# The small weights' loads on the other DMA queue, and a token mix whose first four groups do without the scale

## The chip, the cores and the metric

The kernel runs on one core of a Trainium2 chip. The core has five engines that run side by side and wait for each other by semaphores: TensorE (matmuls, into PSUM), VectorE, ScalarE, GpSimd and SyncE. SyncE (SP) computes nothing here and issues DMAs; ScalarE and GpSimd can issue DMAs too. The metric is the device time of one execution in microseconds. The kernel before takes 497.24 us, the median of 3 runs (497.1 to 499.32).

## The reference

The input x has 4 batches of 32 tokens, each an image of 128x128, float32. The layer is computed in two halves.

```
x1 = x + codano(ln_c(x), ...)           # ln_c: normalised along the last axis, eps 1e-6
out = x1 + ffn(ln_t(x1), W, V, ...)     # ln_t: the same with eps 1e-5

codano(x):  tokens = x as 128 images of one channel
  t = instance_norm(tokens)
  k, q, v = fno(t) with 16 heads        # 1x1 skip + spectral conv on the low modes
  p = softmax(q k^T / scale)            # 32x32 per batch and head
  a = fno(p v)                          # 16 heads -> 1 channel
  a = instance_norm(a + tokens)
  m = instance_norm(a)
  m = gelu(fno(m, norm)); m = fno(m, norm)
  return instance_norm(m) + a

ffn(x):  Wx = batch_norm(x W^T, gamma, beta)   # x as 4 x 16384 x 128
  y_t = sigmoid(Wx_t + V y_(t-1)), y_(-1) = 0   # a scan over 16384 steps
```

A Fourier transform along an axis is a matmul with cosines and sines. The whole of the path through attention and its skip is linear in the tokens once the softmax is known, so that for the pixels it is one 128x128 matrix over tokens, C (`cft` is its transpose), and instance norm multiplies each token's row of C by a scale alpha. The kernel calls the product of every pixel with alpha*C the token mix.

## The kernel before

The program is written out by hand as one block per engine, and what stands in a block is done in that order. Nothing is scheduled by a planner. The stages that matter here are these.

**First stage (span 0 to 78).** x is loaded in 8 chunks of 16 token rows (1 MB) on SP's queue (L472). VectorE takes each row's mean and variance (`ln_moments`, L1162), ScalarE the root (`root`, L947), VectorE the coefficients (`ln_coefs`, L1181, L1182, semaphore ln_coef). VectorE works on chunk c+1 before it gives the coefficients of chunk c. The rows are normalised in place, in each chunk some by ScalarE (L984: 12, 8 and then 4 rows) and the rest by GpSimd (L571: 4, 8 and then 12). TensorE multiplies the normalised rows with a Fourier basis (L625, semaphore rs_filled) and ScalarE copies the result to `rs` (`move_rs`, L388). SP writes the normalised rows to DRAM as xn_rows (L479), since later they are needed with tokens on the partitions; it waits there for both engines' normalised rows, and its queue is in order.

In the same time the weights are prepared. ScalarE issues 27 small DMAs first (L963 to L970); waits for six of them (w_in); scales the projection weights (L973); waits for four transposes of key and query weights and the transposes of W and V that TensorE has made (L977 to L979); and only then takes the first root. GpSimd copies the key and query weights (L539), waits for L973 (wy_skip) and multiplies value and projection weights (L556 to L566), before its first normalised row. The product goes to DRAM, wy_rows (L482), and comes back 16 times, spread over partitions (L488).

After the last chunk TensorE makes `rx`, the row spectra (L625, 128x512), that ScalarE and VectorE copy out (L388) into the place of x's chunks 4 and 5; for this they wait for the DMA that wrote these out (xn_4_5).

**Middle (78 to 139).** Low modes of all tokens, scores, softmax and the products of attention. TensorE fills its gaps with Gram matrices of the spectra: `low_gram` over 32 products, `gram(b, q0, q1)` over 32 per batch b. `gram(b, ...)` reads `rs` of batch b, in whose place xn_rows is read back as x_t, tokens on partitions (L510): chunks 2b and 2b+1, for which SP waits until batch b's Gram is whole (semaphore gram).

**Token mix (139 to 183).** VectorE gets the variance and asks ScalarE for a root (L945), and has alpha; it spreads it over partitions with a diagonal matrix `dg` (L1309) that TensorE multiplies with ones (semaphore bc_filled); `acft` = cft times alpha (L1314). For each of 32 groups of 4 tokens' columns, GpSimd (L584) or, in each fourth group, ScalarE (L1039) gathers the columns into one of five buffers, TensorE multiplies them with `acft` into one of PSUM's banks 4 to 7 (mix_filled), and ScalarE copies the bank to `a0` (L1053). Two things stand inside these 32 groups: TensorE waits behind group 3 for the diagonal of kappa (kap_dg, L1317), and ScalarE ahead of its copy of group 6 waits for zw, the mixer's product (L1322 to L1327 on VectorE), to square and sum it (L1049). From group 24 on TensorE also transposes z3_1.

**Rest (183 to 500).** The two mixers, the second normalisation, W, batch norm, and the scan.

## Time and profile before

| | us |
|---|---|
| median of 3 runs | 497.24 |
| profiled execution | 501.7 |
| its span, first to last instruction | 499.9 |
| TensorE busy | 360.9 (72%) |
| VectorE busy | 364.0 (73%) |
| ScalarE busy | 263.2 (53%) |
| GpSimd busy | 258.3 (52%) |

The profile is one execution. PE is TensorE, PEld its weight loads, DVE VectorE, ACT ScalarE, POOL GpSimd, SP SyncE; ACTq and SPq are the queues on which they issue DMAs. A line such as L571 is a line of the kernel before; matmuls pass through the helpers L625 and L629, and so all carry these. A float32 matmul counts as two passes in the rows' "x". The mean busy shares do not say which engine sets the end, since each stage has its own; the chain of waits does: it goes back from the last instruction, at each step to what released it. "[idle <-X]" at a row's end is the time in which the engine stood still before it, and who ended that.

### The profile page before, as it was taken

How to read it: one execution, taken by the hardware profiler on the slowest of the kernel's cores; microseconds unless marked ns; L12 is line 12 of the kernel's file. 1: busy time of each engine (PE TensorE's matmuls, PEld its weight loads, DVE VectorE, ACT ScalarE, POOL GpSimd, SP SyncE). 2: the span in 40 equal slices, each digit the busy share in tenths (PEclk: the TensorE clock that was granted, in tenths of full speed). 3: DMA queues.
4: the chain of work that ended last, by engine and by line, in shares of the span. 5: the costliest groups of instructions: out<-in, count | busy, mean ns of one | idle time of the engine just before them, and what ended most of it. 6: DMA issues, size and time to landing. Idle time of an engine off the chain costs nothing.

```text
span 499.9 us, 7077 instructions
## 1 busy us (share of the span) xinstructions
PE 360.9 (72%) x2385; PEld 281.8 (56%) x2385; DVE 364.0 (73%) x954; ACT 263.2 (53%) x530; POOL 258.3 (52%) x292
## 2 busy tenths in 40 slices
PE   0169989998949999899701956667865539697790
PEld 0169958794529998789701834333432227465690
DVE  3589312798967847999799477777778368899790
ACT  0678742520227854555100216888889948598000
POOL 1399940000039949997892567666772299300000
PEclk9989997999968999999955886998799978899796
DMA  8999893987150000035550000000000000000499
GB/s 209 272 305 276 227 304 105 208 314 319 26 207 1 1 1 1 1 112 161 167 155 17 1 0 0 3 0 0 0 2 1 0 1 0 1 2 0 127 286 261
DMA packets 61077, 50.93 MB, mean 102 GB/s; under 512 B 4897, under 2 KB 54481, under 8 KB 60017
## 3 DMA queue, kind: packets, MB, share of 16 engines
q1 hardware_dynamic: 57824, 50.18, 34.5%
q10 hardware_dynamic: 3216, 0.30, 0.6%
q8 instruction: 19, 0.31, 0.2%
q14 instruction: 18, 0.14, 0.1%
HBM read 30.45 MB, written 16.88 MB: 95 GB/s over the span
## 4 chain that ended last, share of the span: by engine, by line
DVE 38%; PE 29%; POOL 14%; ACT 7%; issue 5%; ACTq 3%; DMA 1%; DVEq 0%; SPq 0%
PE PS L625 26%; POOL BIG L571 7%; DVE PS L1475 7%; DVE BIG L1268 4%; DVE SML L1162 4%; PE PS L629 3%; DVE BIG L1443 3%; POOL BIG L611 2%; ACT BIG L1089 2%; POOL BIG L606 2%; ACT SML L388 2%; ACTq L970 2%; DVE SML L1457 2%; DVE BIG L1526 2%; DMA BIG<-xn_rows 1%
## 5 line engine op out<-in xcount | busy, mean ns | idle before, releaser
L625 PE MATMUL PS<-CST,BIG 128*128 128x128 f32 (+6 forms) x994 | 128.9, 322 | 23.4 <-ACT BIG L984 10.3
L625 PEld LDWEIGHTS PS<-CST,BIG 128*128 128x128 f32 (+1 forms) x994 | 114.1, 201 | 42.1 <-issue 12.8
L629 PE MATMUL PS<-CST,BIG 128*128 128x128 f32 (+1 forms) x326 | 54.5, 315 | 62.9 <-DVE BIG L1415 25.4
L629 PEld LDWEIGHTS PS<-CST,BIG 128*128 128x128 f32 (+1 forms) x326 | 44.2, 190 | 85.3 <-issue 54.7
L584 POOL COPY BIG<-BIG 128x512 f32<-128x512 f32 x24 | 30.5, 1324 | 77.6 <-DMA BIG<-xn_rows 74.5
L625 PE MATMUL PS<-BIG 128*128 128x128 f32 (+2 forms) x450 | 55.8, 375 | 2.6 <-DVE BIG L1268 2.1
L1162 DVE BATCH_NORM_STATS2 SML<-BIG 128x6 f32<-128x128 f32 x256 | 53.4, 279 | 5.7 <-DMA BIG<-in_x 4.4
L606 POOL TENSOR_TENSOR BIG<-BIG,SML 128x512 f32<-128x512 f32 x32 | 33.3, 1040 | 42.9 <-DVE SML L1182 27.9
L625 PE MATMUL PS<-BIG,SML 128*128 128x256 f32 (+3 forms) x214 | 48.4, 436 | 5.8 <-ACT BIG L1110 5.8
L388 ACT ACTIVATE BIG<-PS 128x512 f32<-128x512 f32 (+3 forms) x59 | 33.1, 572 | 34.2 <-PE PS L625 26.7
L625 PEld LDWEIGHTS PS<-BIG 128*128 128x128 f32 (+2 forms) x450 | 42.8, 175 | 13.2 <-issue 8.4
L1089 ACT ACTIVATE BIG<-BIG,SML 128x128 f32<-128x128 f32 x112 | 46.0, 482 | 3.8 <-DVE SML L1182 3.8
L596 POOL TENSOR_TENSOR BIG<-BIG 128x512 f32<-128x512 f32 x32 | 43.2, 1369 | 6.8 <-DMA BIG<-in_x 6.2
L1475 DVE SCALAR_TENSOR_TENSOR PS<-BIG,SML,PS 128x256 f32<-128x256 f32 x92 | 41.5, 489 | 5.3 <-PE PS L625 5.2
L625 PE MATMUL PS<-SML 128*128 128x512 f32 (+2 forms) x74 | 40.6, 643 | 4.5 <-DVE SML L1500 3.9
L625 PEld LDWEIGHTS PS<-BIG,SML 128*128 128x128 f32 (+1 forms) x214 | 31.2, 186 | 21.0 <-ACT BIG L1110 5.9
L618 POOL TENSOR_TENSOR BIG<-BIG,SML 128x512 f32<-128x512 f32 x32 | 31.9, 1039 | 17.3 <-ACT BIG L1089 17.3
L611 POOL TENSOR_TENSOR BIG<-BIG 128x512 f32<-128x512 f32 x32 | 40.6, 1271 | 0.0
L571 POOL TENSOR_SCALAR BIG<-BIG,SML 128x128 f32<-128x128 f32 x84 | 36.8, 447 | 0.0
L1121 ACT ACTIVATE BIG<-PS,SML 128x256 f32<-128x256 f32 x80 | 35.6, 473 | 1.1 <-DVE PS L1475 0.8
L590 POOL TENSOR_TENSOR BIG<-BIG,SML 128x512 f32<-128x512 f32 x32 | 32.0, 1034 | 7.0 <-ACT BIG L1053 7.0
L1443 DVE TENSOR_TENSOR BIG<-BIG,PS 128x512 f32<-128x512 f32 x32 | 21.7, 678 | 18.5 <-POOL BIG L611 16.9
(210 smaller groups left out, 541.6 us busy)
## 6 DMA issues: line engine op xcount, KB each, us to landing
xn_rows<-BIG SPq DMA_DIRECT2D x8, 1024.0 KB, 7.4
BIG<-xn_rows SPq DMA_DIRECT2D x8, 1024.0 KB, 8.0
BIG<-in_x SPq DMA_DIRECT2D x32, 256.0 KB, 3.0
out_x<-BIG SPq DMA_DIRECT2D x32, 256.0 KB, 3.6
BIG<-wy_rows SPq DMA_DIRECT2D x16, 192.0 KB, 5.4
BIG<-BIG SPq DMA_DIRECT2D x16, 192.0 KB, 4.0
BIG<-in_L_conv_mixer_w SPq DMA_DIRECT2D x2, 544.0 KB, 6.4
CST<-in_const SPq DMA_DIRECT2D x1, 547.5 KB, 8.8
```

Source lines behind the costliest of these rows:

```text
L388: return e.activation(o, i, ACT.Copy) if e is scalar_engine else e.tensor_copy(o, i)
L571: last = pool.tensor_scalar(x_h[:, n, :], x_h[:, n, :], ln_r[:, n:n + 1], ln_b[:, n:n + 1], ALU.mult, ALU.add)
L596: pool.tensor_tensor(v, v, stage[:, g % 3, :, :], ALU.add).then_inc(S("xa"), 1)
L606: pool.tensor_tensor(m1[:, v, :], m1[:, v, :], bet[:, v].unsqueeze(2).to_broadcast([128, 4, W]), ALU.mult).then_inc(S("bm1"), 1)
L611: pool.tensor_tensor(a0[:, v, :], a0[:, v, :], m1[:, v, :], ALU.add).then_inc(S("xm"), 1)
L625: return pe.matmul(o, l, rhs, start=start, stop=stop, **k)
L629: return pe.matmul(o, i, ident[0:n, 0:n], is_transpose=True, start=True, stop=True)
L1089: last = act.activation(m1[:, n, :], a0[:, n, :], ACT.Identity, scale=ln_r[:, n:n + 1], bias=ln_b[:, n:n + 1])
L1121: act.activation(at(y_s, g, i * 2 + (j0 + dj)), sums(g, dj), ACT.Sigmoid, bias=s("bb")).then_inc(S("state"), 1)
L1162: last = dve.bn_stats(ln_st[:, c % 2, row, :], src[:, XR * c + row, :])
L1443: TT(v, v, halves(4 + g % 4), ALU.add).then_inc(S("x1"), 1)
L1475: STT(sums(b, dj), wx_step[:, b, :, bass.ds(j, 1), :], s("bs"), sums(b, dj), ALU.mult, ALU.add).then_inc(S("vy_wx"), 1)
```

## The change

1. Of ScalarE's 27 loads four are left, the two skip weights first, then projection and value weights. The other 23 go to SP's queue: key, query, W and V behind x's chunk 2 (semaphore ffn_in), the 17 rows of parameters four at a time behind chunks 3 to 7, gamma and beta behind them, ahead of the second part of the constants.
2. GpSimd's copies of key and query weights move from its beginning behind chunk 3's rows, TensorE's six transposes behind chunk 4's products, ScalarE's copies of them behind the spectra of chunk 4.
3. The Gram semaphore counts halves of a batch, and SP reads x_t back chunk by chunk.
4. xlow's transposes stand behind 8 products of `low_gram`, not 14.
5. The mix's groups 0 to 3 are multiplied with `cft`, into banks 4, 5, 0 and 1, groups 0 and 1 ahead of TensorE's wait for `dg`. VectorE copies alpha (`al_bc`) and multiplies the four banks by it on their way to `a0` (a0_dve). Groups 4 to 31 go on as before with `acft`. The wait for kap_dg now stands behind group 4, and ScalarE's root of alpha stands ahead of its wait for x_t.

ScalarE's start before, in its own order: all loads stand ahead of the table load and of L973, which scales the projection weights.

```order
L963 DMA BIG<-in_L_conv_proj_w 16x1088
L963 DMA BIG<-in_L_conv_value_w 16x288
L963 DMA BIG<-in_L_conv_key_w 16x288
L963 DMA BIG<-in_L_conv_query_w 16x288
L963 DMA BIG<-in_L_conv_value_skip_w 16x1
L963 DMA BIG<-in_L_conv_proj_skip_w 16x1
...
L970 DMA BIG<-in_L_conv_value_skip_w 128x16
L970 DMA BIG<-in_L_conv_proj_skip_w 128x16
L973 ACT_TABLE_LOAD
L973 ACTIVATE BIG<-BIG 16x16x32 [waits w_in]
L973 ACTIVATE BIG<-BIG 16x16x32
L977 ACTIVATE BIG<-PS 128x64 [waits wt_filled]
```

And after:

```order
L987 DMA BIG<-in_L_conv_value_skip_w 16x1
L988 DMA BIG<-in_L_conv_proj_skip_w 16x1
L989 DMA BIG<-in_L_conv_proj_w 16x1088
L990 DMA BIG<-in_L_conv_value_w 16x288
L993 ACT_TABLE_LOAD
L993 ACTIVATE BIG<-BIG 16x16x32 [waits w_in]
L993 ACTIVATE BIG<-BIG 16x16x32
L978 ACT_TABLE_LOAD
L978 ACTIVATE SML<-SML 128x16 [waits root_of]
L1000 ACTIVATE BIG<-BIG,SML 128x128 [waits ln_coef]
L1000 ACTIVATE BIG<-BIG,SML 128x128 x11
L978 ACTIVATE SML<-SML 128x16 [waits root_of]
```

Gone from between are 23 loads and the three copies that waited for wt_filled; the first root (L978) follows L993 at once.

On SP's queue, before, eight loads of x followed each other, then the constants and the first three writes of normalised rows; the diff shows what now stands between them.

TensorE at the start of the mix before (each group is a row that waits and a row of three more):

```order
L625 MATMUL PS<-SML,CST 128x128 [waits dg]
L625 MATMUL PS<-SML,BIG 128x128 [waits x_mix_pool,acft]
L625 MATMUL PS<-SML,BIG 128x128 x3
L625 MATMUL PS<-SML,BIG 128x128 [waits x_mix_pool]
L625 MATMUL PS<-SML,BIG 128x128 x3
L625 MATMUL PS<-SML,BIG 128x128 [waits x_mix_pool]
L625 MATMUL PS<-SML,BIG 128x128 x3
L625 MATMUL PS<-SML,BIG 128x128 [waits x_mix_act]
L625 MATMUL PS<-SML,BIG 128x128 x3
L625 MATMUL PS<-SML,CST 128x128 [waits kap_dg]
L625 MATMUL PS<-SML,BIG 128x128 [waits x_mix_pool,a0]
L625 MATMUL PS<-SML,BIG 128x128 x3
```

And after:

```order
L643 MATMUL PS<-SML,BIG 128x128 [waits x_mix_pool,cx]
L643 MATMUL PS<-SML,BIG 128x128 x3
L643 MATMUL PS<-SML,BIG 128x128 [waits x_mix_pool]
L643 MATMUL PS<-SML,BIG 128x128 x3
L643 MATMUL PS<-SML,CST 128x128 [waits dg]
L643 MATMUL PS<-SML,BIG 128x128 [waits x_mix_pool]
...
L643 MATMUL PS<-SML,BIG 128x128 [waits x_mix_act]
L643 MATMUL PS<-SML,BIG 128x128 x3
L643 MATMUL PS<-SML,BIG 128x128 [waits x_mix_pool,a0_dve,acft]
L643 MATMUL PS<-SML,BIG 128x128 x3
L643 MATMUL PS<-SML,CST 128x128 [waits kap_dg]
L643 MATMUL PS<-SML,BIG 128x128 [waits x_mix_pool,a0_dve]
```

Two groups stand ahead of the wait for dg and two behind it, and the wait for kap_dg moved from behind the fourth group to behind the fifth.

On VectorE, the copy of alpha and the four multiplications stand between `acft` and the chain to kappa's diagonal; behind that come the six products that make zw.

The diff, without the lines around each place:

```diff
@@ -52,6 +52,7 @@
+WT_AFTER = 4
@@ -62,6 +63,7 @@
+MIX_EARLY = 4
@@ -243,6 +245,7 @@
+        al_bc = BIG3[:, 1664:1792]
@@ -343,6 +346,9 @@
+        def mix_bank(g):
+            return (4, 5, 0, 1)[g] if g < MIX_EARLY else 4 + g % 4
@@ -470,6 +476,17 @@
+                if c == 2:
+                    sp.dma_start(wcp[:, 1376:1664], t["key_w"].rearrange("o n h w v -> n (o h w v)")).then_inc(S("ffn_in"), 16)
+                    sp.dma_start(wcp[:, 1664:1952], t["query_w"].rearrange("o n h w v -> n (o h w v)")).then_inc(S("ffn_in"), 16)
+                    sp.dma_start(w_t, t["W"]).then_inc(S("ffn_in"), 16)
+                    sp.dma_start(v_t, t["V"]).then_inc(S("ffn_in"), 16)
+                if c >= 3:
+                    rows = [(n, *at) for n, at in ROW_AT.items() if at[1] <= NH]
+                    for name, a, size in rows[4 * c - 12:4 * c - 8]:
+                        sp.dma_start(PRM[:, a:a + size], flat(t[name]).to_broadcast([128, size])).then_inc(S("prm"), 16)
+            sp.dma_start(s("gamma"), t["gamma"].unsqueeze(1)).then_inc(S("gamma_in"), 16)
+            sp.dma_start(s("beta"), t["beta"].unsqueeze(1)).then_inc(S("gamma_in"), 16)
@@ -504,8 +521,7 @@
-                if c % 2 == 0:
-                    sp.wait_ge(S("gram"), c // 2 + 1)
+                sp.wait_ge(S("gram"), c + 1)
@@ -533,12 +549,8 @@
-            pool.wait_ge(S("w_in"), 16 * 6)
+            pool.wait_ge(S("w_in"), 16 * 4)
-            for k, (wt, part) in enumerate(((w_qry, 0), (w_qry, 1), (w_key, 0), (w_key, 1))):
-                last = pool.tensor_copy(qk_c[:, k, :, :], wt[:, :, 1:9, part].rearrange("n h w -> n w h"))
-            last.then_inc(S("qk_c"), 1)
@@ -572,6 +584,11 @@
+                if c == WT_AFTER - 1:
+                    pool.wait_ge(S("ffn_in"), 16 * 4)
+                    for k, (wt, part) in enumerate(((w_qry, 0), (w_qry, 1), (w_key, 0), (w_key, 1))):
+                        end = pool.tensor_copy(qk_c[:, k, :, :], wt[:, :, 1:9, part].rearrange("n h w -> n w h"))
+                    end.then_inc(S("qk_c"), 1)
@@ -583,7 +600,8 @@
-            pool.wait_ge(S("a0"), 32)
+            pool.wait_ge(S("a0"), 32 - MIX_EARLY)
+            pool.wait_ge(S("a0_dve"), MIX_EARLY)
@@ -634,16 +652,10 @@
-                if q1 == 32:
-                    last.then_inc(S("gram"), 1)
+                    if q % 16 == 15:
+                        last.then_inc(S("gram"), 1)
-            pe.wait_ge(S("ffn_in"), 16 * 4)
-            pe.wait_ge(S("qk_c"), 1)
-            for k in range(4):
-                tr(PS[:, 4, 16 * k:16 * k + 16], qk_c[:, k, :, :])
-            tr(PS[:, 5, 0:128], w_t)
-            tr(PS[:, 5, 128:256], v_t).then_inc(S("wt_filled"), 1)
@@ -656,6 +668,13 @@
+                if c == WT_AFTER:
+                    pe.wait_ge(S("ffn_in"), 16 * 4)
+                    pe.wait_ge(S("qk_c"), 1)
+                    for k in range(4):
+                        tr(PS[:, 4, 16 * k:16 * k + 16], qk_c[:, k, :, :])
+                    tr(PS[:, 5, 0:128], w_t)
+                    tr(PS[:, 5, 128:256], v_t).then_inc(S("wt_filled"), 1)
@@ -690,11 +709,11 @@
-            low_gram(0, 14)
+            low_gram(0, 8)
-            low_gram(14, 32)
+            low_gram(8, 32)
@@ -759,8 +778,24 @@
+            def mix(g, c):
+                if g % MIX_ACT == MIX_ACT - 1:
+                    pe.wait_ge(S("x_mix_act"), (g + 1) // MIX_ACT)
+                else:
+                    pe.wait_ge(S("x_mix_pool"), g + 1 - (g + 1) // MIX_ACT)
+                for w in range(4):
+                    last = mm(PS[:, mix_bank(g), 128 * w:128 * w + 128], x_mix[:, g % MIX_RING, w, :], c)
+                last.then_inc(S("mix_filled"), 1)
+            pe.wait_ge(S("cx"), 1)
+            mix(0, cft)
+            mix(1, cft)
+            mix(2, cft)
+            mix(3, cft)
@@ -782,17 +817,13 @@
-            for g in range(32):
-                if g >= 4:
-                    pe.wait_ge(S("a0"), g - 3)
-                if g % MIX_ACT == MIX_ACT - 1:
-                    pe.wait_ge(S("x_mix_act"), (g + 1) // MIX_ACT)
-                else:
-                    pe.wait_ge(S("x_mix_pool"), g + 1 - (g + 1) // MIX_ACT)
-                for w in range(4):
-                    last = mm(PS[:, 4 + g % 4, 128 * w:128 * w + 128], x_mix[:, g % MIX_RING, w, :], acft)
-                last.then_inc(S("mix_filled"), 1)
-                if g == 3:
+            for g in range(MIX_EARLY, 32):
+                if g < MIX_EARLY + 2:
+                    pe.wait_ge(S("a0_dve"), g - MIX_EARLY + 1)
+                if g >= MIX_EARLY + 4:
+                    pe.wait_ge(S("a0"), g - MIX_EARLY - 3)
+                mix(g, acft)
+                if g == MIX_EARLY:
@@ -805,7 +836,7 @@
-            pe.wait_ge(S("a0"), 32)
+            pe.wait_ge(S("a0"), 32 - MIX_EARLY)
@@ -953,30 +984,15 @@
-            for name, a, n, src in (
-                    ("w_in", 0, 1088, t["proj_w"].rearrange("n o h w v -> n (o h w v)")),
-                    ("w_in", 1088, 288, t["value_w"].rearrange("o n h w v -> n (o h w v)")),
-                    ("w_in", 1376, 288, t["key_w"].rearrange("o n h w v -> n (o h w v)")),
-                    ("w_in", 1664, 288, t["query_w"].rearrange("o n h w v -> n (o h w v)")),
-                    ("w_in", 1952, 1, t["value_skip_w"].rearrange("o n -> n o")),
-                    ("w_in", 1953, 1, t["proj_skip_w"])):
-                act.dma_start(wcp[:, a:a + n], src).then_inc(S(name), 16)
-            act.dma_start(w_t, t["W"]).then_inc(S("ffn_in"), 16)
-            act.dma_start(v_t, t["V"]).then_inc(S("ffn_in"), 16)
-            act.dma_start(s("gamma"), t["gamma"].unsqueeze(1)).then_inc(S("ffn_in"), 16)
-            act.dma_start(s("beta"), t["beta"].unsqueeze(1)).then_inc(S("ffn_in"), 16)
-            for name, (a, n) in ROW_AT.items():
-                if n <= NH:
-                    act.dma_start(PRM[:, a:a + n], flat(t[name]).to_broadcast([128, n])).then_inc(S("prm"), 16)
-            act.wait_ge(S("w_in"), 16 * 6)
+            act.dma_start(wcp[:, 1952:1953], t["value_skip_w"].rearrange("o n -> n o")).then_inc(S("w_in"), 16)
+            act.dma_start(wcp[:, 1953:1954], t["proj_skip_w"]).then_inc(S("w_in"), 16)
+            act.dma_start(wcp[:, 0:1088], t["proj_w"].rearrange("n o h w v -> n (o h w v)")).then_inc(S("w_in"), 16)
+            act.dma_start(wcp[:, 1088:1376], t["value_w"].rearrange("o n h w v -> n (o h w v)")).then_inc(S("w_in"), 16)
+            act.wait_ge(S("w_in"), 16 * 4)
-            act.wait_ge(S("wt_filled"), 1)
-            act.activation(aqk.rearrange("m k n -> m (k n)"), PS[:, 4, 0:64], ACT.Copy)
-            act.activation(w_t, PS[:, 5, 0:128], ACT.Copy)
-            act.activation(v_t, PS[:, 5, 128:256], ACT.Copy).then_inc(S("wt"), 1)
@@ -989,6 +1005,11 @@
+                if c == WT_AFTER + 1:
+                    act.wait_ge(S("wt_filled"), 1)
+                    act.activation(aqk.rearrange("m k n -> m (k n)"), PS[:, 4, 0:64], ACT.Copy)
+                    act.activation(w_t, PS[:, 5, 0:128], ACT.Copy)
+                    act.activation(v_t, PS[:, 5, 128:256], ACT.Copy).then_inc(S("wt"), 1)
@@ -1019,7 +1040,7 @@
-            act.wait_ge(S("gram"), 4)
+            act.wait_ge(S("gram"), 2 * NB)
@@ -1038,9 +1059,9 @@
+            root(s("al"), s("rt"))
-            root(s("al"), s("rt"))
@@ -1049,10 +1070,13 @@
-                act.wait_ge(S("mix_filled"), g + 1)
-                act.activation(a0[:, :, 4 * g:4 * g + 4],
-                               PS[:, 4 + g % 4, :].rearrange("h (w t) -> h t w", w=4), ACT.Copy).then_inc(S("a0"), 1)
+                if g >= MIX_EARLY:
+                    act.wait_ge(S("mix_filled"), g + 1)
+                    act.activation(a0[:, :, 4 * g:4 * g + 4],
+                                   PS[:, mix_bank(g), :].rearrange("h (w t) -> h t w", w=4), ACT.Copy).then_inc(S("a0"), 1)
+                    if g + MIX_ACT >= MIX_RING:
+                        act.wait_ge(S("mix_filled"), g + MIX_ACT + 1 - MIX_RING)
@@ -1312,6 +1336,11 @@
+            link(dve.tensor_copy(al_bc, PS[:, 6, 384:512]))
+            for g in range(MIX_EARLY):
+                dve.wait_ge(S("mix_filled"), g + 1)
+                TT(a0[:, :, 4 * g:4 * g + 4], PS[:, mix_bank(g), :].rearrange("h (w t) -> h t w", w=4),
+                   al_bc.unsqueeze(2).to_broadcast([128, NT, 4]), ALU.mult).then_inc(S("a0_dve"), 1)
@@ -1463,6 +1492,7 @@
+            dve.wait_ge(S("gamma_in"), 32)

```

## Rows read from the trace of the kernel before

**Rows 1.** The page, chain that ended last, shares by line:
```profile
PE PS L625 26%; POOL BIG L571 7%; DVE PS L1475 7%; DVE BIG L1268 4%; DVE SML L1162 4%; PE PS L629 3%; DVE BIG L1443 3%; POOL BIG L611 2%; ACT BIG L1089 2%; POOL BIG L606 2%; ACT SML L388 2%; ACTq L970 2%; DVE SML L1457 2%; DVE BIG L1526 2%; DMA BIG<-xn_rows 1%
```

**Rows 2.** The chain in order of time (start us, us, what):
```profile
14.98 0.72 ACTq L970
...
17.02 2.37 ACT BIG L973 x2
...
31.19 36.81 POOL BIG L571 x84
```

**Rows 3.** Timeline 0 to 60 (start us, us, engine, line):
```profile
3.06 0.44 ACTq L963 DMA_DIRECT2D BIG<-in_L_conv_proj_skip_w  x1
...
8.68 1.40 POOL L539 COPY SML<-BIG 16x128 f32<-16x128 f32 x4 [8.24 <-DMA BIG<-in_L_conv_proj_skip_w]
...
12.12 1.20 PE L629 MATMUL PS<-CST,SML 16*128 16x16 f32 x6 [12.12 <-DMA SML<-in_L_ffn_beta]
...
12.58 3.19 DVE L1162 BATCH_NORM_STATS2 SML<-BIG 128x6 f32<-128x128 f32 x16 [0.22 <-DMA BIG<-in_x]
...
21.95 4.74 ACT L984 ACTIVATE BIG<-BIG,SML 128x128 f32<-128x128 f32 x12 [0.53 <-DVE SML L1182]
...
28.46 3.19 DVE L1162 BATCH_NORM_STATS2 SML<-BIG 128x6 f32<-128x128 f32 x16
```

**Rows 4.** DMA: queue, issues (last: us to landing), issue times in ns, one issue:
```profile
q10 hardware_dynamic: 3216, 0.30, 0.6%
...
BIG<-in_x SPq DMA_DIRECT2D x32, 256.0 KB, 3.0
...
CST<-in_const SPq DMA_DIRECT2D x1, 547.5 KB, 8.8
...
L472 SPq DMA_DIRECT2D BIG<-in_x x8: 864/3374/4438, 1.3 to 25.6; - x8
...
9.54 0.96 ACTq L970 DMA_DIRECT2D BIG<-in_L_conv_mixer_out_g  x1
```

**Rows 5.** Timeline: a row of SP's queue, and ScalarE's first rx copy:
```profile
47.04 5.58 SPq L479 DMA_DIRECT2D xn_rows<-BIG  x2
...
71.08 0.60 ACT L388 ACTIVATE BIG<-PS 128x512 f32<-128x512 f32 x1 [1.07 <-PE PS L625]
```

**Rows 6.** Stretches: PE, PEld, DVE, ACT, POOL busy, PEclk, DMA, GB/s:
```profile
68.00:77.80 9.80, 8.79 (x46) 3.90 (x46) 3.64 (x10) 3.28 (x7) 0.14 (x1) 1.00 1.11 320
...
147.60:153.50 5.90, 5.88 (x31) 5.88 (x32) 5.49 (x11) 1.95 (x4) 3.74 (x1) 0.58 0.00 0
...
159.80:172.90 13.10, 13.10 (x120) 13.10 (x119) 8.45 (x8) 11.41 (x21) 13.10 (x12) 1.00 0.01 1
```

**Rows 7.** Timeline: Low Gram, scores, and the chain's last x_t landing:
```profile
82.74 5.91 PE L625 MATMUL PS<-BIG 64*128 64x128 f32 x28
...
96.63 3.64 PE L625 MATMUL PS<-BIG,SML 128*32 128x512 f32 x32
...
135.51 7.01 DMA BIG<-xn_rows
```

**Rows 8.** Timeline of alpha and the mix, and L1443 from the page:
```profile
143.93 0.75 DVE L1157 TENSOR_TENSOR SML<-SML,BIG 128x1 f32<-128x1 f32 x1
144.72 1.01 DVE L1309 TENSOR_SCALAR SML<-CST,SML 128x128 f32<-128x128 f32 x1
...
148.48 0.29 DVE L1317 TENSOR_SCALAR SML<-CST,SML 128x128 f32<-128x128 f32 x1
...
154.35 1.57 DVE L1327 TENSOR_TENSOR BIG<-BIG 128x512 f32<-128x512 f32 x1
...
156.35 1.05 ACT L1049 ACTIVATE BIG<-BIG 128x1024 f32<-128x1024 f32 x1
...
153.87 4.41 PE L625 MATMUL PS<-SML,BIG 128*128 128x128 f32 x38
...
L1443 DVE TENSOR_TENSOR BIG<-BIG,PS 128x512 f32<-128x512 f32 x32 | 21.7, 678 | 18.5 <-POOL BIG L611 16.9
```

## Prediction

> **What bounds the kernel now.** I read first the by-line shares of the chain of waits [rows 1]. TensorE's matmuls hold a quarter, but next stands one line of GpSimd, L571. So I opened the chain in order of time [rows 2]: ScalarE's queue issues small loads until 15.7, loads a table, scales the weights (L973, to 19.4), and only then GpSimd starts the weight products that occupy it up to 31.19. From there L571 runs 36.8 us with no gap. The end of the first stage (68.0) is therefore set by how early ScalarE gets through its queue, not by x. The timeline [rows 3] shows the same from the other side: VectorE has finished the statistics of chunk 1 at about 16.5 and starts chunk 2 only at 21.95, since the first root comes late on ScalarE. The second place of the change is the token mix. There TensorE has a queue of 256 passes; from 159.8 it is full (13.10 of 13.10 us), and before that it waits for alpha and then runs its first 32 passes at a granted clock of 0.58, the lower of its levels for most of the time [rows 6, 8].
>
> **The sum is made on the profiled execution:** span 499.9 us, 501.7 us measured. The median of the runs shown is 497.24, 0.9% lower; I take the differences over unscaled. All times below are on the clock of the trace before.
>
> **A. ScalarE's queue is cut to four loads.** An issue costs 0.44 us with 0.03 between, and six ended at 3.50 [rows 3], so with four ScalarE is through at 2.6, and the table load (1.28) is done by 3.9. L973 then waits for w_in. The skip weight, the slowest, now is issued first; before, GpSimd's copies that wait for the same loads started at 8.68, 5.6 after the last of them was issued at 3.06 [rows 3]. So it lands between 4.6 and 6.8; I take 6.8. L973 takes 2.37 -> 9.2. GpSimd's products take 31.19-19.46 = 11.7 -> 20.9, which is 10.2 earlier.
> GpSimd then needs coefficients. Chunk 0's are ready after VectorE's second chunk of statistics (12.58+3.19 and 0.8 of small operations, plus 0.5: 17.1), because x_in1 arrives at 12.5 [rows 3]. ScalarE normalises its 12 rows in 4.74, to 21.8, and gives root 1 behind them; VectorE's coefficients 1 stand at 22.6, and coefficients 2 one chunk later. A chunk takes VectorE 28.46 to 32.9, 4.4 us: 27.1. GpSimd, which would be ready for chunk 2 at 20.9+12x0.438 = 26.2, waits 0.9 us. From chunk 2 on 72 instructions of 0.44 (36.81/84) make 31.6, and the four copies of key and query weights, moved here in front of chunk 4, add 1.4 [rows 3]. GpSimd ends at 27.1+31.6+1.4 = 60.1; half a microsecond for VectorE's small operations waiting behind GpSimd's makes it 60.6. **Term A: -7.4.** Bounds: -8.8 (nothing waits after 20.9: 20.9+36.8+1.4 = 59.1) and -4.6 (L973 a further 2.8 late). The six transposes of key, query, W and V (1.20 us, at 12.12 before [rows 3]) move into TensorE's chunk 4; TensorE has two light chunks (6 and 7) behind it to catch up in, so I take 0 to 0.7, and 0.
>
> **B. SP's queue takes 23 loads between x's chunks.** Behind each stand x's next chunk, the second part of the constants, and the writes of the normalised rows. An x chunk takes SP 3.37 us to issue in the median but 0.86 when the queue is empty [rows 4], so SP is waiting for transfers already, and 2 to 4 issues of 0.45 fit into that wait. What they move is small: the whole ScalarE queue, 3216 packets, took 0.6% of the span, 3.0 us. VectorE needs chunks 4 to 7 at 27, 32, 36 and 40, and the eighth issue ended at 29.0 before; so even 21x0.47 = 9.9 us of pure delay lets GpSimd's later chunks through. What could suffer is the write of chunks 4 and 5, which the rx copies wait for. They are issued as GpSimd gets done with a chunk, the fourth at 47.04 [rows 5]. Now all come 7 us earlier, but the transfers of x and constants end no earlier than before (the last x issue started at 25.6 and took about 3.4, the constants follow and land 8.8 later: 37.8 [rows 4]). At the 320 GB/s of the stretch with the fullest queues [rows 6] a 1 MB write takes 3.3 us. Four of them bring the landing that releases the five wy loads to 51; with chunk 4, those loads (1 MB in all) and itself, chunk 5 lands at about 62; the rx copies want it at 71.08-7.4 = 63.7. Before, those copies waited for TensorE and not for the transfer [rows 5]. **Term B: 0**, up to +3.8 if the 9.9 us are not hidden (SP free at 43.6, chunk 5 landed at 67.5).
> The Trainium skill (DMA: Bandwidth & Descriptors, Issuing engines are not separate DMA queues) says that SP's and ScalarE's DMAs run on the same 16 engines and that a second issuer only saves issue time. By that rule the move costs x at most issue time; the 3.0 us of small packets are there either way.
>
> **C. Low Gram 8 instead of 14 first.** Six Low Gram products, 12 of 28 passes in 5.91 us, so 2.5 us, no longer stand ahead of xlow's transposes [rows 7]. But the same passes stand ahead of the score matmuls (96.63) in either order, and TensorE has hardly a gap up to there. **-0.2**, at most -2.5.
>
> **D. x_t in single chunks and the early mix.** Before, the last two chunks were issued together and were 7.0 us on their way, to 142.5 [rows 7]. Now only one is left for then. A 256 KB load lands in 3.0 [rows 4]; the slope from there to 2 MB in 7.0 is 2.3 us per MB. So x_t is complete at 140.1, not 142.5. GpSimd begins copying at 140.1, and that is while VectorE works out alpha. In the trace its operations with two SBUF inputs end on GpSimd's boundaries when a copy runs: the multiplication by g took 0.75 instead of 0.16, L1309 1.01 where L1317 took 0.29 [rows 8]. Copies from 140.1 on have their boundaries near 141.1, 142.1, 143.15, 144.2 and 145.2. VectorE's two updates of q end behind 142.1 and 143.15; then 0.15, the root 0.2 (it no longer stands behind ScalarE's column copy of 1.1) and the reciprocal 0.16, the product with g behind 144.2, the diagonal behind 145.2. Before it ended at 145.73: alpha is 0.5 earlier, and so is alpha*C (147.1).
> Then VectorE gets five operations more ahead of the kappa chain: the copy of alpha, 0.3, and four multiplications from PSUM of 0.68 (the 128x512 row of L1443, [rows 8]), 3.1 us with the links. Kappa's diagonal, at 148.77 before, is at 151.5. TensorE has done groups 0 to 4 by 149.8 and waits for it at group 4 (before it stood behind group 3 and cost nothing). Group 5 starts at 151.9, 2.9 earlier than before.
> The products that end in zw take 7.15 us after the diagonal: 158.7, not 155.9. **ScalarE waits for zw at group 6**, in its queue ahead of all further copies. Before, it arrived at 156.35, just as zw was there [rows 8]. Now it arrives 3 to 4 us too early and stands still: square 1.24, copies 6 and 7 1.07, columns of group 11 1.09 -> 162.1. TensorE starved for group 11 starts it at 162.1, where before it started at 160.2 (153.87, where group 4 began, and seven groups of 0.9). From there it is full as before (a group is 8 passes, 0.87 to 0.9). **Term D: +2.0.** Bounds: -5.1 (group 5 at 149.7 instead of 154.8 and no hold) and +5 (three more of VectorE's chained operations wait a full copy of 1.03).
> The Trainium skill (SBUF — State Buffer, SBUF: two separate sides) states an exclusive lock on the shared port pair for a whole instruction, against VectorE operations with two SBUF inputs. The trace agrees (0.75 and 1.01, above). Without such a lock alpha would be another 0.7 to 1.2 earlier and D about +1.
>
> **Sum:** -7.4 + 0 - 0.2 + 2.0 = -5.6. 497.24 - 5.6 = **491.6 us**. The rest of the kernel shifts as a whole; gamma and beta land hundreds of microseconds before they are read.
>
> **Rivals.**
> *The mix pays in full (chance 0.12).* If zw and kappa come in time, D is -5.1: -7.4-0.2-5.1 = -12.7, 484.5 us. For it: TensorE's 32 slow passes really leave the path. Against: the order of VectorE's queue, in which 3 us are put in front of zw.
> *The small loads hold x's stream (0.07), slower.* If a small load blocks SP's queue for the 0.96 us that some issues took on ScalarE's [rows 4], 21 of them add up to 20 us: SP is free at 52, the writes queue behind it, chunk 5 lands near 77 and the rx copies, at 71.1 before, end 4.1 later. With D +2.0 and C: +5.9, 503 us. It decides from a landing of chunks 4 and 5 at about 71. Against: those 0.9 rows stand for four of 27 loads, and SP's short first issue.
> *Both stages disappoint (0.15):* A -5, D +5, 497 us, no change that can be told. For it: many short chained operations of VectorE beside GpSimd.
> *B half hidden (0.13):* -7.4+3-0.2+2, 494.6.
> The forecast itself has 0.53, with 489 to 494.5 as its own range.
>
> **How the numbers follow.** About 0.5% (2.5 us) is what a measurement can tell from no change: below 494.75, above 499.7. Faster: nearly all of the forecast (0.50), the full mix 0.12, half of "half hidden" 0.07, 0.02 of the disappointment: 0.71. Slower: 0.07 and a tail of the disappointment, 0.09. Same: 0.20. The range goes from near the full mix to past the no-change case: 485.5 to 498.
>
> **What would show it.** A: L973 starts near 7, the run of 84 begins at 21 and ends at 60 to 61, with short waits for coefficients; if it ends after 63, A failed. B: SP's const issue ends before 36 and the rx copies again wait for TensorE; if they wait for xn_rows, B failed. D: x_t complete 2.4 us earlier relative to L1297's end; TensorE waiting for kappa's diagonal behind group 4; ScalarE waiting about 3 to 4 us for VectorE's zw before its square. If ScalarE does not wait there, the full mix is right. The forecast is wrong if the end of the mix (182.9 before) does not come 5 to 6 us earlier, or if a later stage takes another length.

## The result and the profile after

| | kernel before | changed kernel |
|---|---|---|
| median, first comparison | 498.13 (11 runs) | 494.37 (11 runs) |
| median, second comparison | 498.49 (16 runs) | 495.77 (12 runs) |
| profiled execution | 501.7 | 493.59 |
| its span | 499.9 | 491.8 |

The ratio is 0.9905 (95%: 0.9876 to 0.9933), and 0.9932 (0.9891 to 0.9973) in the second comparison: some 3.4 to 4.7 us faster. The ratios leave out executions that lie more than 1.5% above the fastest of the same kernel, which are two of 11 and two of 12 of the changed kernel's and six of 12 in experiment 4. 491.6 was predicted, from 497.24 for the kernel before.

The two profiled executions differ by 8.1 us, twice as much. To see what of this belongs to the change, stage boundaries were read from each trace of this study. "Scaling" is the start of the first scaling behind the residual Gram (L1000 before, L1021 after), "mask" the end of L1297 and L1321, "mix" the start of GpSimd's kappa products (L608 of the changed kernel), "bet" the start of its products with `bet` (L624), all in us; in brackets the time since the boundary on the left. Each is rounded by itself, so a difference can be off by 0.1.

| trace | scaling | mask | mix | bet | span |
|---|---|---|---|---|---|
| before, first | 82.9 | 140.6 (57.6) | 183.2 (42.7) | 280.1 (96.9) | 499.9 (219.8) |
| before, second | 81.9 | 137.2 (55.3) | 180.4 (43.2) | 275.7 (95.3) | 495.3 (219.6) |
| changed, first | 75.0 | 130.5 (55.5) | 177.0 (46.5) | 271.0 (94.0) | 491.8 (220.8) |
| changed, second | 75.6 | 132.9 (57.3) | 180.5 (47.6) | 276.7 (96.2) | 496.2 (219.5) |
| Low Gram split at 14 | 74.9 | 130.2 (55.3) | 175.5 (45.3) | 273.1 (97.6) | 493.7 (220.6) |
| no early mix | 74.6 | 130.1 (55.5) | 172.1 (42.0) | 269.4 (97.3) | 490.0 (220.6) |
| old start | 82.3 | 137.8 (55.5) | 185.3 (47.5) | 281.5 (96.2) | 501.0 (219.5) |
| ScalarE's waits later | 74.8 | 130.2 (55.4) | 170.8 (40.6) | 266.3 (95.5) | 486.9 (220.6) |
| all three waits later | 75.1 | 130.6 (55.5) | 172.0 (41.4) | 267.4 (95.4) | 486.8 (219.4) |

Up to the scaling the change gains 6.3 to 7.9 us (7.0 and 7.1 up to stage 2's first product, 69.89 and 69.76 before, 62.81 and 62.72 after). In the mix it loses 3.3 to 4.9 in these two pairs; the two other kernels with the same mix, those with the Low Gram split at 14 and with the old start, have 45.3 and 47.5, so that the loss over all four is 2.1 to 4.9. Between scaling and mask nothing but scatter lies. The traces scatter by more than the gain: the changed kernel's second one (496.2) ends 0.9 us behind the second one of before (495.3).

The start, in the timeline of the changed kernel (start us, us, engine, line, operation; in brackets the idle time before and who ended it). These answer to [rows 2, 3, 5]:

```profile
9.14 0.62 POOL L568 TENSOR_TENSOR BIG<-BIG 16x128 f32<-16x128 f32 x1 [8.70 <-ACT BIG L993]
...
20.80 1.80 POOL L583 TENSOR_SCALAR BIG<-BIG,SML 128x128 f32<-128x128 f32 x4
23.58 3.51 POOL L583 TENSOR_SCALAR BIG<-BIG,SML 128x128 f32<-128x128 f32 x8 [0.98 <-DVE SML L1206]
28.01 10.47 POOL L583 TENSOR_SCALAR BIG<-BIG,SML 128x128 f32<-128x128 f32 x24 [0.92 <-DVE SML L1206]
38.43 1.42 POOL L590 COPY SML<-BIG 16x128 f32<-16x128 f32 x4
39.84 21.07 POOL L583 TENSOR_SCALAR BIG<-BIG,SML 128x128 f32<-128x128 f32 x48
60.87 0.19 POOL L592 MEMSET BIG<- 128x128 f32 x1
...
62.81 3.65 PE L643 MATMUL PS<-BIG,CST 128*64 128x512 f32 x16 [0.57 <-ACT BIG L394]
64.23 0.60 ACT L394 ACTIVATE BIG<-PS 128x512 f32<-128x512 f32 x1 [1.29 <-DMA xn_rows<-BIG]
64.87 0.69 DVE L394 COPY BIG<-PS 128x512 f32<-128x512 f32 x1 [1.35 <-PE PS L643]
```

GpSimd's run of rows begins at 20.80 where it began at 31.19, 10.4 earlier. It now stands still twice for VectorE's coefficients (the first of them waited in turn 1.01 us for ScalarE's root, which stands behind ScalarE's 12 rows) and has the copies of key and query weights in it, so it ends at 60.9 where it ended at 68.0: 7.1 of the 10.4 are left. ScalarE's first rx copy now waits for the written rows and not for TensorE, 1.42 us behind the first product where before it was 1.19 (71.08 against 69.89). VectorE's first, at 64.87, still waits for TensorE, so the 0.2 us go no further.

SP's queue of the changed kernel (the third column names the queue; what the row shows is the time until it had issued), which answers to [rows 4]:

```profile
8.07 3.51 SPq L480 DMA_DIRECT2D BIG<-in_L_conv_key_w  x1
...
13.20 0.71 SPq L478 DMA_DIRECT2D BIG<-in_x  x1
13.95 1.97 SPq L487 DMA_DIRECT2D BIG<-in_L_conv_norm_g  x1
15.96 0.43 SPq L487 DMA_DIRECT2D BIG<-in_L_conv_attn_norm_g  x1
...
30.84 0.71 SPq L478 DMA_DIRECT2D BIG<-in_x  x1
31.59 2.34 SPq L487 DMA_DIRECT2D BIG<-in_L_conv_proj_skip_w  x1
...
34.92 0.43 SPq L490 DMA_DIRECT2D CST<-in_const  x1
```

The time that x's chunks used to take to issue (3.37 in the median) has passed to the first small load behind each of them (1.6 to 3.5 us); the chunk itself takes 0.71, the other small loads 0.43. The constants start to be issued 5.9 us later than before, at 34.92, and their issue ends at 35.35 where it ended at 32.82. Nobody misses them, and from x's third chunk on VectorE waits for x in neither kernel.

The token mix of the changed kernel, its timeline from alpha on, for [rows 8]:

```profile
129.87 6.09 POOL L601 COPY BIG<-BIG 128x512 f32<-128x512 f32 x6 [68.81 <-DMA BIG<-xn_rows]
...
134.00 1.02 DVE L1333 TENSOR_SCALAR SML<-CST,SML 128x128 f32<-128x128 f32 x1
...
137.09 2.48 DVE L1342 TENSOR_TENSOR BIG<-PS,BIG 128x512 f32<-128x512 f32 x4
...
141.23 0.28 DVE L1346 TENSOR_SCALAR SML<-CST,SML 128x128 f32<-128x128 f32 x1
...
141.57 0.49 PE L643 MATMUL PS<-SML,CST 128*128 128x128 f32 x2 [1.70 <-DVE SML L1346]
141.89 4.63 PE L643 MATMUL PS<-SML,BIG 128*128 128x128 f32 x40
...
143.01 7.98 POOL L601 COPY BIG<-BIG 128x512 f32<-128x512 f32 x4 [2.03 <-PE PS L643]
...
147.09 1.53 DVE L1356 TENSOR_TENSOR BIG<-BIG 128x512 f32<-128x512 f32 x1
148.66 1.06 ACT L1070 ACTIVATE BIG<-BIG 128x1024 f32<-128x1024 f32 x1 [5.07 <-DVE BIG L1356]
...
150.34 7.85 PE L643 MATMUL PS<-SML,BIG 128*128 128x128 f32 x42 [3.82 <-ACT BIG L1075]
```

ScalarE stands 5.07 us at its square of zw, VectorE's last product before it being L1356. Its copies of groups 6 and 7 stand behind the square, and TensorE's group 10 needs the bank of group 6. TensorE has eaten what ScalarE had emptied for it, stands 3.82 us, and resumes at 150.34. What it resumes with is in the stretches (engines in the order of [rows 6], then the granted clock):

```profile
141.90:146.50 4.60, 4.60 (x42) 4.43 (x40) 4.57 (x5) 0.60 (x1) 3.49 (x1) 1.00 0.00 0
150.30:155.00 4.70, 4.66 (x22) 4.66 (x23) 1.03 (x4) 3.74 (x7) 1.51 (x2) 0.50 0.00 0
155.00:160.00 5.00, 5.00 (x40) 5.00 (x40) 2.02 (x5) 3.70 (x7) 3.49 (x4) 0.86 0.00 0
160.00:176.00 16.00, 16.00 (x146) 16.00 (x146) 10.07 (x12) 11.74 (x19) 9.48 (x9) 1.00 0.01 3
```

Behind the idle time TensorE runs at 0.50, the lower of its levels (1.2 GHz): 22 passes in 4.66 us, 0.21 each, where it needs 0.11 at full clock.

The length of this hold is not the same in each execution. In the second trace of the changed kernel two of VectorE's six products took 2.0 us instead of 1.1, beside GpSimd's copies, and ScalarE stood longer:

```profile
146.06 2.00 DVE L1353 TENSOR_TENSOR BIG<-BIG 128x512 f32<-128x512 f32 x1
...
152.89 1.06 ACT L1070 ACTIVATE BIG<-BIG 128x1024 f32<-128x1024 f32 x1 [6.79 <-DVE BIG L1356]
```

In the first trace L1353 was short:

```profile
143.56 1.10 DVE L1353 TENSOR_TENSOR BIG<-BIG 128x512 f32<-128x512 f32 x1
```

Over the four traces with this mix ScalarE stood 4.0, 5.1, 6.8 and 6.8 us, TensorE behind it 2.2, 3.8, 5.5 and 5.5, and the mix took 45.3, 46.5, 47.5 and 47.6: the longer the hold, the longer the mix.

### The profile page after: what moved, and what is told of

The parts are those of the page before. It is cut to its first block, busy times and chain, and to the rows that moved or that the text cites. A ratio compares the mean times of both kernels' runs of the same rounds, so it can differ in the third digit from the quotient of the medians.

```text
span 491.8 us, 7081 instructions
## 1 busy us (share of the span) xinstructions
PE 358.8 (73%) x2385; PEld 279.8 (57%) x2385; DVE 365.3 (74%) x959; ACT 260.8 (53%) x526; POOL 258.5 (53%) x292
## 4 chain that ended last, share of the span: by engine, by line
DVE 42%; PE 28%; POOL 13%; ACT 9%; issue 4%; DMA 1%; DVEq 0%; SPq 0%; ACTq 0%; POOLq 0%
PE PS L643 24%; DVE PS L1505 7%; POOL BIG L583 6%; DVE BIG L1292 6%; DVE SML L1186 5%; PE PS L647 4%; ACT BIG L1113 3%; DVE BIG L1472 2%; POOL BIG L608 2%; ACT SML L394 2%; POOL BIG L629 2%; DVE BIG L1556 2%; POOL BIG L624 2%; DVE SML L1486 2%; DMA BIG<-in_x 1%
## 5 line engine op out<-in xcount | busy, mean ns | idle before, releaser
L643 PE MATMUL PS<-CST,BIG 128*128 128x128 f32 (+6 forms) x994 | 126.5, 319 | 31.4 <-ACT BIG L1000 19.9
L643 PEld LDWEIGHTS PS<-CST,BIG 128*128 128x128 f32 (+1 forms) x994 | 111.5, 197 | 49.9 <-issue 32.7
L647 PEld LDWEIGHTS PS<-CST,BIG 128*128 128x128 f32 (+1 forms) x326 | 44.5, 189 | 81.4 <-issue 53.5
L643 PE MATMUL PS<-BIG 128*128 128x128 f32 (+2 forms) x450 | 53.5, 368 | 2.6 <-DVE BIG L1292 2.1
L624 POOL TENSOR_TENSOR BIG<-BIG,SML 128x512 f32<-128x512 f32 x32 | 33.3, 1042 | 40.0 <-DVE SML L1206 27.9
L394 ACT ACTIVATE BIG<-PS 128x512 f32<-128x512 f32 (+3 forms) x59 | 32.4, 571 | 29.8 <-PE PS L643 21.5
L643 PEld LDWEIGHTS PS<-BIG 128*128 128x128 f32 (+2 forms) x450 | 40.6, 168 | 13.0 <-issue 8.2
L636 POOL TENSOR_TENSOR BIG<-BIG,SML 128x512 f32<-128x512 f32 x32 | 32.0, 1041 | 17.3 <-ACT BIG L1113 17.3
L629 POOL TENSOR_TENSOR BIG<-BIG 128x512 f32<-128x512 f32 x32 | 40.6, 1271 | 0.0
L643 PE MATMUL PS<-SML,BIG 128*128 128x128 f32 (+1 forms) x264 | 35.4, 298 | 5.2 <-ACT BIG L1075 3.8
L643 PEld LDWEIGHTS PS<-SML,BIG 128*128 128x128 f32 (+1 forms) x264 | 34.3, 213 | 6.2 <-ACT BIG L1075 4.0
```

The costliest lines, as they stand in the source:

```text
L394: return e.activation(o, i, ACT.Copy) if e is scalar_engine else e.tensor_copy(o, i)
L624: pool.tensor_tensor(m1[:, v, :], m1[:, v, :], bet[:, v].unsqueeze(2).to_broadcast([128, 4, W]), ALU.mult).then_inc(S("bm1"), 1)
L629: pool.tensor_tensor(a0[:, v, :], a0[:, v, :], m1[:, v, :], ALU.add).then_inc(S("xm"), 1)
L636: pool.tensor_tensor(a0[:, v, :], a0[:, v, :], g0[:, v].unsqueeze(2).to_broadcast([128, 4, W]), ALU.add).then_inc(S("x1_g0"), 1)
L643: return pe.matmul(o, l, rhs, start=start, stop=stop, **k)
L647: return pe.matmul(o, i, ident[0:n, 0:n], is_transpose=True, start=True, stop=True)
```

## Experiments

All ratios are against the kernel before, run beside them on the same chip. The first four share one set of its runs (median 498.01 of 29), the next four another (498.49 of 16), the last four a third (498.76 of 11).

**1. The Low Gram split undone.** `low_gram(0, 14)` and `low_gram(14, 32)` again.

> The changed kernel with one part undone: the Low Gram passes are again split at group 14, as in the kernel before; the new start and the early mix stay. The changed kernel was 4.7 us faster than the one before, and its trace gained 3.0 us between the first residual copy and the mask (10.08 us ahead there, 7.08 at stage 2's start), where the prediction had 0.2. Theory: the reorder made these 3 us, by keeping TensorE supplied while the clock of the kernel before fell to 0.56 at 77.8 to 88.4 us. Then this kernel loses 2.5 to 3 us against the changed one (ratio to before 0.995 to 0.997) and its trace shows a granted clock under 0.9 in the Low Gram. Rival: the dip belonged to that one execution or to other work (DMA), then this kernel stays within 0.5 us of the changed one (ratio 0.990) at a clock near 1.0 there.

Measured: 0.9941 (0.9918 to 0.9964), median 495.13. The two theories give 0.996 and 0.990, and the time lies between them; the traces decide. Scaling to mask takes 55.3 us with the split at 14 and 55.5 with 8. TensorE in that kernel:

```profile
74.77 3.58 PE L643 MATMUL PS<-BIG 64*128 64x128 f32 x28
```

The 28 passes take 3.58, where they took 5.91 in the first trace of before [rows 7]. The reorder is not what saved the time. What this kernel has over the changed one in its trace is a stretch at half clock elsewhere, after the mix (0.50 from 180 to 190, 97.6 us to `bet` against 94.0). Its median is 0.8 us over the changed kernel's in the first comparison and 0.6 under it in the second.

**2. The early mix undone.** Alpha's root stands behind ScalarE's first column copy, all 32 groups are multiplied with `acft`, VectorE's five operations are gone.

```diff
-            link(dve.tensor_copy(al_bc, PS[:, 6, 384:512]))
-            for g in range(MIX_EARLY):
...
-                if g == MIX_EARLY:
...
+                if g == 3:
                     pe.wait_ge(S("kap_dg"), 1)
```

> The changed kernel with the early mix undone: alpha's root stands behind the mix's columns again, the first four groups are multiplied with the diagonal that kappa is in, nothing is scaled at the copies; the new start, x transposed by chunk and the Low Gram split at 8 stay. Theory: the early mix costs 2 to 4 us (the trace of the changed kernel lost 3.8 us between the mask and the mix's end), so this kernel is 2 to 4 us faster than the changed one: 486 to 488 where before has 497, ratio 0.980 to 0.985. It keeps the earlier landing of x_t (2.7 us between mask and GpSimd's copies). Rival: the early groups are worth what they fill of TensorE's wait, then this kernel is slower than the changed one by 1 to 3 us, ratio 0.993 to 0.997.

Measured: 0.9866 (0.9814 to 0.9917), median 491.4. In the trace the mix takes 42.0 us instead of 46.5 and 47.6, so the early mix costs 4.5 to 5.6 (3.3 against the shortest of the four traces that have it). ScalarE's wait at the square is 1.3 us, not 5.07, though two of VectorE's products were long here too. By the ratios the time falls only by 2 to 3. This trace has a stretch at half clock behind the mix (0.50 from 175 to 185, 97.3 to `bet`); whether the other executions had one is not known. The ratio lies just above the 0.980 to 0.985 expected.

**3. The old start.** All loads on ScalarE, key and query weights first on GpSimd, the rest as in the changed kernel.

> The changed kernel with the start of the kernel before: all small loads on ScalarE's queue, q and k copied and transposed ahead of x's statistics; x transposed by chunk, the Low Gram split at 8 and the early mix stay. Theory: the start is worth 7.1 us, handed on undiminished, so this kernel is 7 us slower than the changed one: 1.5 to 3 us slower than before, ratio 1.003 to 1.006 (early mix +3.8 us and middle -3 us against before, if the middle's gain is the reorder's, so down to 1.000). Rival: part of the start's gain is given back later (x's last groups waited for), then this kernel is only 4 to 5 us slower than the changed one, ratio 0.998 to 1.001.

Measured: 1.005 (1.0012 to 1.0088), median 501.44: by the ratios 5.9 to 7.2 us over the changed kernel. GpSimd's run and all behind it are where they were:

```profile
31.50 36.77 POOL L576 TENSOR_SCALAR BIG<-BIG,SML 128x128 f32<-128x128 f32 x84
```

The scaling starts at 82.3 against 75.0. The start's 7.1 us are handed on whole. And what is left of the change without it is by the ratio 2.5 us slower than before (0.6 to 4.4): the price of the mix's term in the time itself.

**4. All three waits later.** ScalarE's and TensorE's.

```diff
-                if g == MIX_EARLY:
+                if g == MIX_EARLY + 4:
                     pe.wait_ge(S("kap_dg"), 1)
...
-                if g == 6:
+                if g == 11:
                     act.wait_ge(S("zw"), 1)
...
-                if g == 14:
+                if g == 17:
                     root(s("r1"), s("rt"))
```

> The changed kernel with its early mix kept and three waits put where what they wait for is ready: ScalarE's square of zw behind group 11 of the first product's copies (was 6), its root behind group 17 (was 14), and TensorE's wait for kappa's diagonal four groups later, so that eight groups are multiplied with C alone before the queue stands (was four). Theory: what the early mix costs is these holds (ScalarE stood 5.07 us at the square, TensorE 3.82 us, and ran at a granted clock of 0.50 for the 4.7 us behind it). Without them the mask-to-mix-end stretch is 4 to 6 us shorter than in the changed kernel: 487 to 489 where before has 497, ratio 0.979 to 0.984, and the clock behind the diagonal stays above 0.8. Rival: the mix is bound by VectorE's chain to kappa's and zw's ends, whatever stands in the queues, then this kernel is within 1 us of the changed one, ratio 0.989 to 0.992.

Measured: 0.987 (0.9822 to 0.9919), above the 0.979 to 0.984 expected. Its 12 times lie between 487.1 and 499.8 with a median of 493.99, so the time alone is unclear. The mix takes 41.4 us in the trace, 5 less than in the changed kernel, as expected. ScalarE still stands 3.44 us at its square, and the granted clock is 1.00 behind the diagonal but 0.77 from 147 to 152. Groups 4 to 8 are multiplied with `acft` here too; what moved is TensorE's wait alone.

**5. The kernel before, profiled again.**

> The kernel before, unchanged, profiled a second time. In its first profile 56.4 us passed from the first of the six scalings behind the residual Gram (82.9 us) to the mask's end; in the changed kernel, with the Low Gram split at 8 or at 14, and with the old start and the split at 8, it was 53.9 to 54.3 us, and none of these four shows the granted clock under 1.0 between 78 and 88 us (there 0.66). Theory: the fall of the clock there was an event of that one execution; then this profile has 54.1 us in that stretch, a clock of 1.0 at 78 to 88 us, and if it falls elsewhere the 3 us are lost there; time 496 to 499. Rival: the old start together with the split at 14 brings the fall each time; then it is here again, at 56.4 us.

Measured: 497.11 us, within the 496 to 499 expected. TensorE in the middle of this second trace, beside [rows 7]:

```profile
81.75 3.58 PE L625 MATMUL PS<-BIG 64*128 64x128 f32 x28
```

and its stretch there:

```profile
77.00:87.00 10.00, 9.54 (x82) 9.10 (x81) 3.25 (x9) 3.88 (x13) 0.00 (x0) 1.00 0.27 69
```

In the first trace of the same kernel that stretch was:

```profile
78.00:88.00 10.00, 10.00 (x58) 9.62 (x59) 1.10 (x5) 2.93 (x9) 0.00 (x0) 0.66 0.17 36
```

The clock is 1.00 instead of 0.66, and scaling to mask takes 55.3 instead of 57.6. From stage 2's first product (69.76) to the mask it is 67.5 us, in the first trace 70.6, in the changed kernel 67.7. So all of the 3.0 us that the first pair of traces seemed to gain there belongs to that one execution of the kernel before. Against this second trace the changed kernel's first is 3.5 us ahead at the end, near the 3.8 and 2.7 of the medians.

**6. The changed kernel again.**

> The changed kernel, unchanged, on this chip again, to set the others of this call against and for a second trace. Expected ratio 0.990 with an interval that overlaps the first one (0.988 to 0.993). If TensorE's half clock falls in at a place that differs from execution to execution, this trace's milestones agree with the first within 0.5 us up to the mask and differ by 2 to 4 us where a fall lies (175 to 190 us, as in two other kernels, or none); if the place belongs to the kernel, both traces agree throughout.

Measured: 0.9932 (0.9891 to 0.9973), median 495.77. Its trace shows the same event in the same place:

```profile
70.00:78.00 8.00, 7.55 (x47) 6.96 (x45) 1.20 (x7) 2.39 (x8) 0.00 (x0) 0.74 1.09 307
78.00:88.00 10.00, 10.00 (x77) 9.76 (x76) 8.01 (x7) 6.82 (x20) 0.00 (x0) 0.87 0.79 168
```

57.3 us from scaling to mask, 1.8 over the others, with the Low Gram split at 8. So the clock can fall in this stretch with either split, and mostly does not: in two of the nine traces of the table, and in none of the other five there. My expectation that the two traces would agree up to the mask was wrong. Counted from stage 2's first product to the mask, the two cost 3.2 us (70.7 against 67.5) and 2.6 (70.2 against 67.7). The stretches behind the mix in experiments 1 and 2 are such events in another place; what they cost can't be told as well, since from mix to `bet` the traces without them have anything from 94.0 to 96.9.

**7. ScalarE's two waits alone.** As 4, without the edit on TensorE.

> The changed kernel with ScalarE's two waits alone moved (square of zw behind group 11 of its copies, was 6; root behind 17, was 14); TensorE's wait for kappa's diagonal stays behind group 4. With all three moved the stretch from the mask to the mix's end took 41.4 us against 46.5 in the changed kernel. Theory: ScalarE's hold (5.07 us at the square, TensorE without work 3.82 us behind it and at half clock for 4.7 us) is most of it: 42 to 43 us here, and the time 2 to 4 us under the changed kernel's. Rival: TensorE's own hold of 1.7 us at the diagonal, with the late refill behind it, is what counts: then 45 us or more.

Measured: 0.9808 (0.9746 to 0.9869), median 488.55. The mix takes 40.6 us, less than the 42 to 43 expected, and the time is by the ratios 4.8 to 6.2 us under the changed kernel's, where 2 to 4 were expected. It is also less than the 41.4 with all three waits moved, but experiment 12 has 40.4 for that kernel, so moving TensorE's wait too shows neither gain nor loss. The timeline of this kernel:

```profile
140.71 0.49 PE L643 MATMUL PS<-SML,CST 128*128 128x128 f32 x2 [1.83 <-DVE SML L1346]
...
141.03 19.66 PE L643 MATMUL PS<-SML,BIG 128*128 128x128 f32 x160
...
148.71 1.05 ACT L1070 ACTIVATE BIG<-BIG 128x1024 f32<-128x1024 f32 x1
```

TensorE still waits 1.83 us for kappa's diagonal, but from 141.03 on runs 160 passes without a break, and ScalarE comes to its square without waiting. Its stretches:

```profile
141.00:145.00 4.00, 4.00 (x23) 4.00 (x23) 3.97 (x5) 1.45 (x3) 2.21 (x1) 0.57 0.00 0
145.00:150.00 5.00, 5.00 (x47) 5.00 (x46) 4.93 (x5) 4.40 (x9) 5.00 (x4) 1.00 0.00 0
150.00:155.00 5.00, 5.00 (x47) 5.00 (x46) 1.50 (x4) 5.00 (x10) 5.00 (x6) 1.00 0.01 3
```

The slow stretch is now one, behind the wait at the diagonal, and no second follows. Moving two waits in ScalarE's queue is worth 5.9 us against the first trace of the changed kernel, and 4.7 to 7.0 against the four traces with the unmoved waits.

**8. Less for GpSimd in chunk 2, on top of experiment 2.** `LN_POOL = [4, 8, 8] + 5 * [12]`, was `[4, 8] + 6 * [12]`.

> The changed kernel without the early mix (ratio 0.987 to before so far), and with GpSimd's share of the statistics' rows cut from 84 to 80 of 128, the four going to ScalarE. Theory of the start's gain: stage 1 ends when GpSimd's unbroken run of rows ends (it began at 20.8 us and ended at 60.9 in the changed kernel), so four rows of 0.45 us less end it up to 1.8 us sooner: the first scaling behind the residual Gram at 73.2 to 73.6 us (74.6 without this edit), time 1 to 1.8 us less, ratio 0.983 to 0.985. Rival: ScalarE or the transfer of x is as late, then nothing moves (within 0.3 us), or ScalarE's four more rows of 0.485 us make it later.

Measured: 0.9845 (0.9784 to 0.9906), median 490.15. The scaling starts at 75.2, with 74.6 without this edit; the 1 us in the time is not from there, so that the expected ratio (0.983 to 0.985) was met by luck. GpSimd:

```profile
28.11 3.51 POOL L579 TENSOR_SCALAR BIG<-BIG,SML 128x128 f32<-128x128 f32 x8 [1.03 <-DVE SML L1186]
32.76 5.25 POOL L579 TENSOR_SCALAR BIG<-BIG,SML 128x128 f32<-128x128 f32 x12 [1.14 <-DVE SML L1186]
...
60.41 0.19 POOL L588 MEMSET BIG<- 128x128 f32 x1
```

The rows taken away left a third wait of 1.14 us for coefficients, ahead of chunk 3. Up to there x's statistics set the pace, as before the cut they did up to chunk 2.

**9. Experiment 7 again.**

> The kernel with ScalarE's two waits moved (square behind group 11, root behind 17), again, to set the next two against and to see whether its ratio of 0.981 to the kernel before holds. Expected 0.978 to 0.987, and 40.4 to 41.5 us from the mask's end to the mix's end (40.6 in its first trace).

Measured: 0.9808 (0.9762 to 0.9854), median 488.86, the mix 40.5 us. The gain holds.

**10. Less for GpSimd in the last chunk, on top of 7.** `LN_POOL = [4, 8] + 5 * [12] + [8]`.

> The kernel with ScalarE's two waits moved, and GpSimd's rows of the last chunk cut from 12 to 8 of 16, four rows going to ScalarE. A cut in chunk 2 moved nothing (GpSimd's run ended at 60.41, 60.51 without it), since GpSimd then waited 1.14 us for x's third set of coefficients. Here no wait lies behind the cut. Theory: the run ends 4 x 0.44 = 1.8 us sooner, but ScalarE's copies, 0.89 us apart and last begun at 60.45, are nearly as late and get 4 x 0.41 us more work: stage 2 starts within 0.5 us of where it did (62.8), time within 1 us. Rival: GpSimd's run alone sets the start of stage 2: then it starts 1.5 to 1.8 us sooner.

Measured: 0.9785 (0.973 to 0.984), median 487.7, the fastest kernel here, though not told apart from experiment 9 by the time. GpSimd's run ends 1.5 us sooner, stage 2's first product comes 0.7 sooner (61.96 against 62.64; up to 0.5 was expected). It is not ScalarE's added rows that are late now, as the expectation had it: ScalarE's last copies each wait 0.29 us for TensorE, and the chain that ended last goes through TensorE's products, 128 passes without a gap from 46.98 to 61.29. GpSimd's end, TensorE and ScalarE in this kernel:

```profile
39.81 19.39 POOL L583 TENSOR_SCALAR BIG<-BIG,SML 128x128 f32<-128x128 f32 x44
...
53.96 7.31 PE L643 MATMUL PS<-CST,BIG 128*128 128x128 f32 x64
...
61.31 0.60 ACT L394 ACTIVATE BIG<-PS 128x512 f32<-128x512 f32 x1 [0.29 <-PE PS L643]
...
64.16 1.24 ACT L394 ACTIVATE BIG<-PS 128x512 f32<-128x512 f32 x2 [2.08 <-DMA xn_rows<-BIG]
```

The last row is the next limit: ScalarE's rx copies wait for the written rows and start at 64.16, as in experiment 9 (64.17).

**11. GpSimd's products made longer, on top of 7.** Two lines of the products twice.

> The kernel with ScalarE's two waits moved, and six of GpSimd's products ahead of its run of rows made twice (4 of 0.62 and 2 of 0.70 us, with their gaps 4.4 us). It prices one microsecond of GpSimd's start. GpSimd waits 0.98 and 1.03 us for the coefficients of chunks 1 and 2 after its run has begun. Theory: the new start freed 10.4 us and only 7.1 arrived since from there on x's statistics are late too: then 2.0 of the 4.4 us are hidden, GpSimd's run and stage 2 are 2.4 us later (63.1 and 65.2), time 2 to 2.5 us more (ratio 0.986). Rival one: GpSimd's run sets it throughout, all 4.4 us arrive. Rival two: the run isn't what stage 2 waits for, under 1 us arrives.

Measured: 0.9871 (0.9811 to 0.9932), median 491.26, 2.4 us over experiment 9. GpSimd:

```profile
25.39 15.73 POOL L585 TENSOR_SCALAR BIG<-BIG,SML 128x128 f32<-128x128 f32 x36
...
42.49 21.14 POOL L585 TENSOR_SCALAR BIG<-BIG,SML 128x128 f32<-128x128 f32 x48
63.58 0.19 POOL L594 MEMSET BIG<- 128x128 f32 x1
```

The run starts 4.7 us later (25.39 against 20.72), both waits are gone from it, and it ends 2.9 later (63.58 against 60.69), as does the scaling (77.7 against 74.8). So 1.8 of 4.7 us were hidden, near the 2.0 that GpSimd had waited. The ratios give 3.1 us instead of the 2.4 of the medians, with four and six executions. TensorE's slow stretch stands behind the wait for alpha in this trace (0.68 and 0.63), as in the changed kernel's first one, and the mix takes 41.0 all the same.

**12. Experiment 4, profiled again.**

> The kernel with all three waits moved, profiled a second time: its first profile (488.6 us, the mix 41.4 us from the mask's end) was among the fastest of runs that lay between 487.1 and 499.8, the median at 494.0. Theory: TensorE's half clock falls into stretches where TensorE sets the time, in another place in each execution; then a run of 492 to 496 us shows one more such stretch than the first (clock under 0.7 over 8 us or more), with the stages outside it equal within 0.5 us. Rival: the later diagonal makes the mix itself vary, then the 4 to 8 us lie between mask and mix end at a clock over 0.9.

Measured: 487.88 us, the mix 40.4 us from the mask. The execution was as short as the first one, so neither theory was put to the test. Why experiment 4 has executions near 495 to 500 stays open.

## Why the prediction was right, and where it was off

491.6 was predicted, with 489 to 494.5 as the forecast's own range; measured was 494.4, just inside it, and 495.8, outside. By the ratios the gain is 3.4 to 4.7 us, not 5.6. The number 494.6 of the rival "B half hidden" is nearer, but not its mechanism: B cost nothing, and what is missing lies in D. The text's own test, the mix's end 5 to 6 us earlier, can't be read from one pair of traces: it comes 6.2 us earlier in the first pair, of which 3 are the fall of the clock in the middle of before, and not at all in the second (180.4 and 180.5), where the fall is in the changed kernel. By its terms:

**A, the start, -7.4: shown, -7.1.** ScalarE's L993 ended at 9.0 (9.2 predicted), the run began at 20.8 (20.9) and ended at 60.9 (60.6), with waits of 0.98 and 0.92 for coefficients (0.9 predicted, one of them). Experiment 3 gives the term as a time, 5.9 to 7.2; experiment 11 shows why 10.4 us at the head of GpSimd's work are worth 7: up to 2 are lost to x's statistics, and 1.4 to the copies of key and query. What L993 waited for was not the skip weight, as the text had it, but the value weight, the last issued, which landed at 6.6.

**B, SP's queue, 0: right in effect, its test missed by 0.2 us.** The text said that B had failed if the rx copies wait for the written rows. ScalarE's first did, some 0.2 us longer than TensorE's product would have held it, and VectorE's first copy behind it still waited for TensorE. The const issue ended at 35.35, before the 36 that the text names. "Small loads hold x's stream" did not come: the issues were dear only behind a chunk, where SP had waited before. The 0.9 us issues that this rival went by are three of the 27, not four.

**C, the Low Gram, -0.2: small as predicted, but +0.2.** The first pair of traces seems to say -3. Experiments 1, 3, 5 and 6 take it away: 55.3 to 55.5 us with either split, and 57.3 and 57.6 where the clock fell, once under each. What is left has the other sign: from stage 2's first product to the mask it is 67.48 us in two traces with the split at 14, and 67.67 to 67.69 in nine with the split at 8; the three traces left, two of them those with the fall, have 68.6 to 70.7. So the new order costs 0.2 us.

**D, the mix, +2.0: the step that was mis-sized, measured +3.3 to +4.9** (46.5 and 47.6 against 42.7 and 43.2), and +2.1 to +4.9 with the two other kernels that have this mix. Its steps were there: x_t 2.7 us earlier against the mask (2.4 predicted), alpha 0.6 (0.5), kappa's diagonal +2.8 (+2.7), zw +2.8 (+2.8), TensorE waiting at the diagonal, ScalarE at the square (5.07, and 4.0 to 6.8 over four traces, with 3 to 4 predicted). Even group 11 starts where the text has it, 21.6 us behind the mask's end (21.5). What failed is the sentence "From there it is full as before". TensorE was full, but at half clock: 22 passes took 4.66 us, 2.2 more than at 0.11 each, 14 of them behind the start of group 11, and from 155 to 160 the clock was still 0.86. In the second trace it is the hold that was longer too: the text put the six products at 7.15 us from the diagonal, and they took 7.1 to 7.2 in some traces and 8.8 to 8.9 in others, of the kernel before (8.9 in its second trace) as well. The first slow stretch, which the prediction did count, stands behind the wait for alpha, and the second one came with the new wait. Experiments 7, 9, 10 and 11 show that the hold is the cause: with ScalarE's square and root put later in its queue, VectorE's work, the diagonal and zw are where they were within 1 us, and the mix takes 40.2 to 41.0 instead of 45.3 to 47.6.

The rival "the mix pays in full" was wrong for this kernel and half right for experiment 7: there D is -2.1 to -2.7, not -5.1, since the wait at the diagonal and one stretch of slow passes remain.

On the lock between VectorE and GpSimd: L1333 again took 1.02 beside a copy where L1346 took 0.28. The other side shows too. GpSimd's column copies took 1.01 each at 129.87 (6.09 for six) and 2.0 each at 143.01 (7.98 for four), most of them under VectorE's products of two SBUF operands; and in the second trace two of these products took 2.0 us instead of 1.1. The Trainium skill (SBUF — State Buffer, SBUF: two separate sides) states an exclusive lock on the shared ports, and these rows agree.

## What to carry to other kernels

When work is added ahead of a result on one engine, look for the engines that wait for that result in the middle of their queue, and move those waits back until the result is there (here by five groups): here the wait, left where it was, turned a gain of some 2 us into a loss of 2 to 5. Price such a hold as the idle time plus the slow passes that followed it on TensorE (granted clock 0.50 to 0.66 for 4.7 us in all four traces). And profile the kernel before twice before a difference between two traces is explained: a stretch of 10 us at a lower clock looked here like 3 us of a gain, and hid that the term had the other sign.

## What was not expected of the hardware

- TensorE's granted clock also fell where it had hardly been idle: 0.66 at 78 to 88 us in the first trace of before with TensorE busy throughout (10.00 of 10.00 us, and 0.46 idle just ahead), and 1.00 there in the second trace of the same kernel. Behind the mix it fell to 0.50 for some 10 us in two of 14 traces. What decides it was not found.
- A load of 18 KB behind a 1 MB chunk held SP's queue for 3.51 us, the three behind it 0.42 each. Interleaving 23 small loads with the large ones mostly moved SP's waiting to another instruction: the issue of x and the constants was through 2.5 us later (35.35 against 32.82), not the 9.9 us that 21 issues of 0.47 add up to.
- The same six products of VectorE took 7.1 to 7.2 us from the diagonal in nine traces and 8.8 to 8.9 in five, also in two traces of one and the same kernel. In all five the third and fourth took 2.0 us instead of 1.1. What decides it was not found.
